# A graph layer and a routed expert layer on one core: set-up reordered, tail of expert tiles reordered, last tables in pieces

## The reference, cut to what matters

```python
# x (128, 128, 256), adj (128, 128, 128): 128 graphs of 128 nodes
def gnn(X, A):                    # X is layernorm(x)
    Xw = X @ Wv + bv
    sj, si = Xw @ aw[:d, 0], Xw @ aw[d:, 0]
    e = leaky_relu(sj[:, None, :] + si[:, :, None] + ab[0], 0.2)
    alpha = A * exp(e)
    T = alpha / (sum(alpha, -1, keepdims=True) + 1e-12)
    H, Xk = 0, X
    for k in range(3):
        H = H + Xk @ Wk[k] + bk[k]
        Xk = einsum('bij,bjd->bid', T, Xk)
    return relu(H)
def ffn(x):                       # x is layernorm(x), 16384 tokens of 256
    probs = softmax(xf @ switch_w.T + switch_b)          # 16 experts
    routes, pos = argmax(probs), rank of the token among those of its expert
    keep = pos < 1228
    y = expert_w[routes] @ token + expert_b[routes]
    return where(keep, y, xf) * max(probs)
x = x + gnn(layernorm(x))
x = x + ffn(layernorm(x))
```

## Time and profile before

| | before |
|---|---|
| median of 3 runs | 777.93 us (775.52 to 778.54) |
| the profiled execution, its own time | 778.68 us |
| its span, first to last instruction | 776.9 us |
| PE busy, PE weight loads busy | 93%, 83% of the span |
| DVE, ACT, POOL busy | 79%, 62%, 55% |
| mean granted clock of TensorE | 0.982 |

### The profile page before, as it was taken

How to read it: one execution, slowest core, us unless ns; L and a number is a source line. 1 busy time by engine, 2 the same in 40 slices (tenths; PEclk the granted TensorE clock), 3 DMA queues, 4 the chain that set the end, 5 groups by cost and what they waited for, 6 DMA issues and landing times.

```text
span 776.9 us, 18809 instructions
## 1 busy us (share of the span) xinstructions
PE 723.0 (93%) x4919; PEld 643.6 (83%) x4919; DVE 611.5 (79%) x2974; ACT 479.7 (62%) x1504; POOL 429.6 (55%) x524
## 2 busy tenths in 40 slices
PE   1999999999999999999999999999999999857883
PEld 1788888888999999999998999989989988746663
DVE  4688888888888888888888888888888887775562
ACT  1456777766666666666666666666666666653551
POOL 5224455556555566566556555665665564565553
PEclk9999999999999999999999999999999999977998
DMA  5723443534443344444434433444443322353430
GB/s 168 205 69 107 136 152 124 177 122 140 144 126 122 126 150 145 144 151 133 145 126 144 142 119 110 142 142 137 145 139 126 103 87 91 98 161 107 123 104 1
DMA packets 92926, 99.76 MB, mean 128 GB/s; under 512 B 10445, under 2 KB 85258, under 8 KB 92822
## 3 DMA queue, kind: packets, MB, share of 16 engines
q1 hardware_dynamic: 77752, 66.36, 28.5%
q0 software_dynamic: 13008, 30.07, 10.8%
q10 hardware_dynamic: 2064, 2.13, 1.0%
HBM read 49.53 MB, written 54.72 MB: 134 GB/s over the span
## 4 chain that ended last, share of the span: by engine, by line
PE 90%; DVE 2%; issue 2%; DMA 2%; SPq 1%; ACT 1%; POOL 1%; POOLq 0%; DVEq 0%; ACTq 0%
PE ps_z12a L1161 12%; PE ps_z12b L1161 11%; PE ps_z0a L1161 9%; PE ps_lgb L1161 9%; PE ps_z0b L1161 8%; PE ps_lga L1255 6%; PE ps_z0b L1262 4%; PE ps_z0a L1262 4%; PE ps_xt L1195 4%; PE ps_z12b L1221 4%; PE ps_xt L1189 4%; PE ps_z12a L1221 3%; PE ps_lgb L1295 3%; PE ps_t L1243 2%; PE ps_t L1212 2%
## 5 line engine op out<-in xcount | busy, mean ns | idle before, releaser
L529 POOL DMA_INDIRECT out<-lent,tok x143 | 145.2, 1016 | 178.2 <-DVE lent L1122 166.7
L512 POOL DMA_INDIRECT rowbuf<-rows,idx x128 | 129.6, 1013 | 55.1 <-issue 27.1
L577 ACT CAST xth<-ps_xt 128x256 fp32r<-128x256 f32 x128 | 47.7, 373 | 137.0 <-PE ps_xt L1195 136.9
L754 DVE TENSOR_TENSOR xtl<-ps_xt,xth 128x256 fp32r<-128x256 f32 x128 | 54.3, 424 | 61.1 <-ACT xft L580 59.7
L651 ACT ACTIVATE x<-rin 128x256 f32<-128x256 f32 x143 | 86.8, 608 | 2.8 <-DMA rin<-rowbuf 2.8
L1255 PEld LDWEIGHTS ps_lga<-swc,xft 128*128 128x128 f32 x512 | 76.5, 190 | 13.9 <-ACT xft L580 3.0
L480 POOL TENSOR_SCALAR x<-xin,nm,r 128x256 f32<-128x256 f32 x128 | 72.3, 565 | 27.2 <-PE ps_xt L1195 16.2
L593 ACT ACTIVATE od<-rows,oc,oa 128x256 f32<-128x256 f32 x128 | 77.0, 602 | 0.1
L476 POOL TENSOR_TENSOR r<-ve,mhalf 128x4 f32<-128x4 f32 x32 | 34.1, 1067 | 77.1 <-ACT ve L623 77.1
L1255 PE MATMUL ps_lga<-swc,xft 128*128 128x16 f32 x512 | 65.8, 242 | 2.6 <-ACT xft L580 2.6
L1195 PE MATMUL ps_xt<-ident,x 128*128 128x128 f32 x256 | 49.5, 276 | 9.2 <-POOL x L480 8.3
(11 more groups left out here) (211 smaller groups left out, 2403.9 us busy)
## 6 DMA issues: line engine op xcount, KB each, us to landing
rin<-rowbuf SPq DMA_DIRECT2D x143, 130.0 KB, 2.1
xin<-in_x SPq DMA_DIRECT2D x32, 512.0 KB, 3.9
out<-od SPq DMA_DIRECT2D x32, 512.0 KB, 4.3
ain<-in_adj SPq DMA_DIRECT2D x32, 256.0 KB, 4.3
ewr<-in_ewT SPq DMA_DIRECT2D x16, 256.0 KB, 2.7
out<-lent,tok POOLq DMA_INDIRECT x143, 2.7
rowbuf<-rin ACTq DMA_DIRECT2D x1, 2080.0 KB, 9.7
rowbuf<-rows,idx POOLq DMA_INDIRECT x128, 3.0
```

Of the source, the lines that this page charges most:

```text
L512: pool.indirect_dma_start(out=rowbuf, out_offset=bass.IndirectOffsetOnAxis(ap=idx[:, i:i + 1], axis=0), in_=rows[:, r, :], in_offset=None, ...
L529: pool.indirect_dma_start(out=out.rearrange("g n d -> (g n) d"), out_offset=bass.IndirectOffsetOnAxis(ap=tok[:, i % RY:i % RY + 1], axis=0 ...
L754: dve.tensor_tensor(xtl[:, g % 2, :], ps_xt[:, 0:D], xth[:, g % 2, :].bitcast(F32), ALU.subtract).then_inc(s_x0l, 1)
```

## The change

Set-up. SP no longer issues the loads of the weights Wk: three loads of 256 KB go out from ACT's queue at its start, each for both halves. The one semaphore `d_w` becomes four. SP then issues the first expert's weights ahead of its wait for the bias rows. ACT runs one Exp on a constant at the start and does its first slots before the two casts of `w12h`. DVE does the statistics of graphs 0 and 1 ahead of its wait for the small vectors, moves the bias rows to the end of the set-up, behind the statistics of graph 4, and cuts `w12l` in two. POOL runs one `pow` on constants (`first`) ahead of its tables of constants and of the memset of `ebp` (line 553). PE waits for `bvb` later.

Tail. PE does `expert(i)` and then `turn(i + 2)`; ACT `high(i + 1)`, `norm(i + 2)`; DVE `low(i + 1)`, `finish(i)`. For tail tiles the register load of tile i+1 stands among the products of tile i, behind the second, and three values are kept from it with `snap`; woven tiles load theirs where they did, and also with `snap`. `last_step` is cut in three pieces, behind tiles 99 to 101, `last_tiles` in six, behind tiles 102 to 107.

```diff
@@ sync
-            for kt in range(KT):
-                ks = slice(kt * P, (kt + 1) * P)
-                sp.dma_start(w12r[:, kt, 0:D], Wk[2, ks, :]).then_inc(d_w, 16)
-                sp.dma_start(w12r[:, kt, D:2 * D], Wk[1, ks, :]).then_inc(d_w, 16)
-                sp.dma_start(w0r[:, kt, 0:D], Wk[0, ks, :]).then_inc(d_w, 16)
...
             sp.dma_start(ebr[:], eb).then_inc(d_eb, 16)
-            sp.wait_ge(s_vc, KT + 4)
+            load_expert(0)
+            sp.wait_ge(s_bkl, 1)
             sp.dma_start(bkh[1:2, :].bitcast(F32), bkl[0:1, :].bitcast(F32)).then_inc(d_bkh, 16)
             load(2, 2)
-            load_expert(0)
@@ gpsimd
+            pool.tensor_tensor(first[:], onesf[:, 0:G], mhalf[:], ALU.pow)
             pool.iota(done[:], pattern=[[1, E]], base=0, channel_multiplier=0,
@@ scalar
-            act.wait_ge(s_fill, 1)
-
-            act.wait_ge(d_w, 16 * (3 * KT + 4))
-            act.copy(w12h[:], w12r).then_inc(s_wh, 1)
+            w12d = [Wk[2].rearrange("(t p) d -> p t d", p=P), Wk[1].rearrange("(t p) d -> p t d", p=P)]
+            for h in range(2):
+                act.dma_start(w12r[:, :, h * D:(h + 1) * D], w12d[h]).then_inc(d_w12, 16)
+            act.dma_start(w0r[:, :, 0:D], Wk[0].rearrange("(t p) d -> p t d", p=P)).then_inc(d_w0, 16)
+            act.wait_ge(s_pc, 2)
+            act.activation(e1[:, 0, 0:1], onesf[:, 0:1], ACT.Exp)
...
             def tile(i):
+                if i + 1 < NT:
+                    high(i + 1)
                 if i + 2 < NT:
-                    high(i + 2)
-                if i + 3 < NT:
-                    norm(i + 3)
-
-            phase_a(act, slot_fn, -LEAD_STATS, LAG_OUT)
+                    norm(i + 2)
+
+            for k in range(-LEAD_STATS, G - LEAD_STATS + 1):
+                slot_fn(0, k)
+            act.wait_ge(d_w12, 32)
+            for kt in range(KT):
+                act.copy(w12h[:, kt, :], w12r[:, kt, :]).then_inc(s_wh, 1)
+            phase_a(act, slot_fn, G - LEAD_STATS + 1, LAG_OUT)
@@ vector
             def set_up():
...
+                dve.wait_ge(d_w0, 16)
                 dve.wait_ge(s_pe0, 1)
...
                 link(dve.tensor_copy(w0h[:], w0r))
-                link(dve.tensor_tensor(w0l[:], w0r, w0h[:].bitcast(F32), ALU.subtract))
-
+                dve.wait_ge(s_wh, 1)
+                dve.tensor_tensor(w12l[:, 0, :], w12r[:, 0, :], w12h[:, 0, :].bitcast(F32),
+                                  ALU.subtract).then_inc(s_w12l, 1)
+                dve.tensor_tensor(w0l[:], w0r, w0h[:].bitcast(F32), ALU.subtract).then_inc(s_w0l, 1)
+                dve.wait_ge(s_wh, 2)
+                dve.tensor_tensor(w12l[:, 1, :], w12r[:, 1, :], w12h[:, 1, :].bitcast(F32),
+                                  ALU.subtract).then_inc(s_w12l, 1)
...
             def tile(i):
-                if i + 2 < NT:
-                    low(i + 2)
+                if i + 1 < NT:
+                    low(i + 1)
                 finish(i)
+                turn = i - (WOVEN + LAG_ROUTE + 1 - REST - G)
+                if 0 <= turn < 3:
+                    last_step(NG - 1, turn)
+                if 3 <= turn < 9:
+                    last_tiles(turn - 3)
 
             dve.wait_ge(s_pc, 13)
+            for k in range(-LEAD_STATS, -LEAD_STATS + 2):
+                slot_fn(0, k)
             dve.wait_ge(d_v, 16 * 4)
             for t in range(KT):
                 link(dve.tensor_scalar(bvb[:, t, :], onesf[:], bvt[:, t:t + 1], None, ALU.mult))
-
-            for k in range(-LEAD_STATS, -LEAD_STATS + G + 1):
+            for k in range(-LEAD_STATS + 2, -LEAD_STATS + G + 1):
                 slot_fn(0, k)
             set_up()
+            dve.wait_ge(d_x[1], 16)
+            dve.bn_stats(st1[:, G % 2, :], xin[:, G, :]).then_inc(s_st1, 1)
+            bias_rows()
@@ tensor
+            def expert_of(i):
+                pe.wait_ge(s_tab, step_of(i))
+                e = pe.value_load(tab_exp[0:1, i:i + 1], min_val=0, max_val=E - 1)
+                at[i] = [pe.snap(e * EW + t * D) for t in range(KT)], pe.snap(e * D)
+
+            def expert(i, ahead=None):
...
-                pe.wait_ge(s_tab, step_of(i))
-                e = pe.value_load(tab_exp[0:1, i:i + 1], min_val=0, max_val=E - 1)
+                if i < WOVEN:
+                    expert_of(i)
+                w, bias = at.pop(i)
                 pe.wait_ge(b_lo, i + 1)
...
+                    product(y, part, xth[:, c, ts], xtl[:, c, ts], ewh_f[:, bass.ds(w[t], D)],
+                            ewl_f[:, bass.ds(w[t], D)], start=(part == 0 and t == 0))
+                    if ahead is not None and (part, t) == (0, 1):
+                        expert_of(ahead)
...
             def tile(i):
+                expert(i, i + 1 if i + 1 < NT else None)
                 if i + 2 < NT:
                     turn(i + 2)
-                expert(i)
```

More of the change, by code:

```diff
@@ L103, in graph_then_experts @@
         abt = sb("abt", [P, 1])
+        first = sb("first", [P, G])
         cvec = sb("cvec", [P, NV])
@@ L206, in graph_then_experts @@
         d_v = sem("d_v")
-        d_w = sem("d_w")
+        d_w12 = sem("d_w12")
+        d_w0 = sem("d_w0")
+        d_bk = sem("d_bk")
+        d_r = sem("d_r")
+        s_w12l = sem("s_w12l")
+        s_w0l = sem("s_w0l")
+        s_bkl = sem("s_bkl")
         d_bkh = sem("d_bkh")
@@ L636, in slot_fn @@
                 if it * BODY + k == B + 1:
-                    for i in range(3):
+                    for i in range(2):
                         norm(WOVEN + i)
                 if it * BODY + k == B + REST:
-                    for i in range(2):
-                        high(WOVEN + i)
+                    high(WOVEN)
                 i = tailed(it, k)
@@ L814, in slot_fn @@
                 g = k + LEAD_STATS
-                if valid(it, g):
+                if valid(it, g) and it * BODY + g != G:
                     if g % G == 0:
@@ L861, in slot_fn @@
                 if s == B + REST:
-                    for i in range(2):
-                        low(WOVEN + i)
+                    low(WOVEN)
                 i = tailed(it, k)
@@ L866, in slot_fn @@
                     tile(i)
-                if s == B + LAG_ROUTE - 1:
-                    last_step(NG - 1)
-                if s == B + LAG_ROUTE:
-                    last_tiles()
             NRO = 11
@@ L1059, in advanced, with last_step, last_tiles @@
                 dve.tensor_tensor(done[:], want[:], have[:], ALU.min).then_inc(s_pick, 1)
-            def last_step(c):
-                backlog(c)
-                whole_tiles(c)
-                running(c)
-                starts(c)
-                passed(c)
-                rises(c)
-                steps(c)
-                picked(c)
-                tile_rows(c)
-                tile_experts(c)
-                reached(c)
-                limits(c)
-                advanced(c)
-            def last_tiles():
+            def last_step(c, turn):
+                if turn == 0:
+                    backlog(c)
+                    whole_tiles(c)
+                    running(c)
+                    starts(c)
+                    passed(c)
+                if turn == 1:
+                    rises(c)
+                    steps(c)
+                    picked(c)
+                    tile_rows(c)
+                    tile_experts(c)
+                if turn == 2:
+                    reached(c)
+                    limits(c)
+                    advanced(c)
+            def last_tiles(turn):
                 def link(n, ins):
@@ new lines, in last_tiles @@
+                if turn == 3:
+                    link(10, dve.tensor_reduce(base[:], pick, AX_X, ALU.add))
+                    link(11, dve.tensor_tensor(kept[:, 0:E], count, most[:], ALU.min))
+                    link(12, dve.tensor_tensor(fall[:], kept[:, 0:E], kept[:, 1:1 + E], ALU.subtract))
+                if turn == 4:
+                    link(13, dve.tensor_tensor(pick, past, by_expert(fall[:], LASTS), ALU.mult))
+                    link(14, dve.tensor_reduce(stop[:], pick, AX_X, ALU.add))
@@ L1312, in expert @@
                     ts = slice(t * P, (t + 1) * P)
-                    w = bass.ds(e * EW + t * D, D)
-                    product(y, part, xth[:, c, ts], xtl[:, c, ts], ewh_f[:, w], ewl_f[:, w],
-                            start=(part == 0 and t == 0))
-                pe.matmul(y, two_ones[:], ebp[:, bass.ds(e * D, D)], start=False, stop=True,
+                    product(y, part, xth[:, c, ts], xtl[:, c, ts], ewh_f[:, bass.ds(w[t], D)],
+                            ewl_f[:, bass.ds(w[t], D)], start=(part == 0 and t == 0))
+                    if ahead is not None and (part, t) == (0, 1):
+                        expert_of(ahead)
+                pe.matmul(y, two_ones[:], ebp[:, bass.ds(bias, D)], start=False, stop=True,
                           skip_group_check=True).then_inc(b_y, 1)
             def tile(i):
+                expert(i, i + 1 if i + 1 < NT else None)
```

(1 more changed line is left out.)

79 lines of the change are left out of this document (43 added, 36 removed).

## The result

The changed kernel takes 771.16 us (median of 6 runs, 770.63 to 771.57) and the kernel before, measured beside it, 775.71 us: a ratio of 0.9932 (95% interval 0.9915 to 0.9949), 4.6 us by the medians and 5.3 by the ratio. The profiled execution took 771.06 us for a span of 769.3, against 778.68 and 776.9 before. The kernel before was profiled once more later (776.33 us, span 774.6), so of the 7.6 us between the first two profiles 2.4 are the spread of the kernel before.

What follows compares the result with a forecast made beforehand. PE was taken to bound the slots, leaving start, drain and tail to change: -2.1 - 2.0 - 4.6 + 1.7 = -7.0, a forecast median of 771.0 us. Its own range was 767 to 774, the whole range 765.0 to 776.5.

Steps and rivals of the forecast that it cites:

- What bounds the kernel: Whole kernel: PE bounds the slots, so changes count only before the first product, in the drain and between tail tiles.
- The set-up: Start: DVE's chain begins earlier, `xtl` of graph 0 at 19.0 instead of 21.12 us; -2.1 us.
- if landings slip by a microsecond, 1.0: Set-up: lower bound, a gain of only 1.0 us if the loads land a microsecond later.
- The collision: Set-up: `bvb` on DVE meets POOL's `ebp` memset and waits until 10.1 us; without it the gain would be 4.6.
- Products before transposes: Drain: tile 98's products fit in PE's 2.8 us wait, tile 99 starts one tile earlier, at 684.8; -2.0 us.
- Tables in pieces: Drain: DVE's tables spread over tiles 99 to 107, tile 109 starts 20.9 us behind tile 99; -4.6 us.
- The register load: Plain tail loop: load stays uncovered among products, `snap` adds 0.1 us, 1.68 a tile over 33 tiles; +1.7 us.
- Rival two: Plain tail loop: load is hidden, POOL's scatter bounds the tile at 1.28 us; 13 us more gain, 758; chance 0.06.
- The first: Set-up: `bvb` escapes the memset, 2.5 us more gain, 768.5; chance 0.17.
- The third: Drain: the tables' hole is only spread, each piece adds to its tile, -4.6 becomes 0, 775.6; chance 0.17.
- The fourth: Plain tail loop: clock falls and stays low, 2.07 us a tile, 784 over all 33 tiles; chance 0.07.

Runs made afterwards that it cites:

- The last version: Changed kernel with `Wk` behind small vectors, earlier `ebp` memset, bias rows behind `xtl`, earlier loads of graphs 8-15, last row scatters back to back: 764.70 us, ratio 0.9846.
- rows first: Changed kernel with POOL issuing the last group's four row scatters back to back, scatters of finished tiles behind them: 776.71 us, ratio 0.9972.
- two loads: Changed kernel with a second register load of the same number in each tail tile, behind the fifth product: 795.80 us, ratio 1.0223.
- normalisation ahead: Changed kernel with ACT's normalisation one tile further ahead, three tiles normalised ahead of the loop: 778.57 us, ratio 0.9999.

## Why the prediction was right in size and where its steps failed

The prediction was 771.0 us, 7.0 less than the 777.93 known then; the change is worth 4.6 to 5.3 us, and the kernel before measured beside it took 775.71. That 771.0 and 771.16 lie so close is luck: the kernel before came out 2.2 us lower than known, and the gain 1.7 to 2.4 us smaller. The stages, in us, from the three undisturbed profiles (tile 99 means the start of its products):

| stage | before, first | before, second | changed | predicted change |
|---|---|---|---|---|
| to the first product | 21.52 | 20.55 | 19.24 | -2.1 |
| to the last slot's product | 642.87 | 643.09 | 641.93 | 0 |
| to tile 99 | 22.44 | 21.11 | 19.57 | -2.0 |
| to tile 109 | 25.46 | 24.75 | 23.16 | -4.6 |
| to tile 142 | 53.73 | 54.13 | 54.08 | +1.7 |
| to the end of the span | 10.9 | 11.0 | 11.3 | 0 |

Against the first profile the changes add up to -7.6, against the second, which lies nearer the medians, to -5.3. The sum came out near because errors pointed both ways: the pieces gave 2.3 to 3.0 less than their term and the start up to 0.8 less, the plain loop 1.4 to 1.8 more, and the slots gave 0.9 to 1.2 that had no term.

**What bounds the kernel** held: slots bound by PE (299.69 of 300.00 us), the gains at the start and in the drain.

**The set-up, -2.1.** Measured -2.3 between the first profiles, 2.2 on average over twelve: the size was right. The path was not. The prediction had DVE's chain run from the `ebp` memset through the two `bvb` instructions and the statistics. In the traces it runs from the landing of the last small vector through PE: PE's sums for the set-up start when that vector lands (9.49 us in the changed kernel), and DVE's copy of them, `lent_w<-ps_lgb`, comes some 2.85 us behind the landing in all ten profiles with the new set-up, whatever the memset did to `bvb`. With the bias rows ahead of `xtl` the first product comes 9.8 us behind the landing in seven profiles of eight (9.6 in the eighth), with the rows behind it 8.2 in both. The landing was put at 6.5 to 7.5 us and came at 8.3 to 9.6, so "if landings slip by a microsecond, 1.0" was wrong as well: they slipped by more, and the gain stood, since the memset was never in the path. The last version issues `Wk` behind the vectors and has them at 7.02, 2.45 us earlier, and its bias rows, 1.85 us on DVE where the prediction had 1.65, stand behind `xtl`, which is worth the 1.55 between 9.77 and 8.22: these two are its 4.0 us.

The collision itself is real. In the changed kernel's first profile it did not happen, the memset having ended at 9.10; in five others with the same set-up the vectors landed earlier, and the first `bvb`, 0.29 us otherwise, lasted until just behind the memset's end. The second profile of the changed kernel, whose memset ended at 9.11 (timeline of DVE), and the second of the kernel before, whose memset ended at 8.05:

```profile
8.53 0.98 DVE L1163 TENSOR_SCALAR lent<-onesf,bvt 128x128 f32<-128x128 f32 x2 [1.36 <-DMA abt<-in_ab]
```

```profile
6.44 2.01 DVE L1133 TENSOR_SCALAR lent<-onesf,bvt 128x128 f32<-128x128 f32 x2 [6.44 <-DMA abt<-in_ab]
```

The Trainium skill states in "SBUF — State Buffer", section "SBUF: two separate sides", that a DVE instruction in a 2-port mode and one of GpSimd lock each other out for the whole instruction. These runs agree where the other instruction is the memset: 0.98, 2.01 and 2.36 us for the two with overlap, 0.61 without. The last version doesn't show it for the `pow`: there the two took 0.61 us from 7.02, with `first` at work on POOL from 6.69 to 7.73.

The price of the `pow`, 2.01 us, was misread too. In the kernel before it ran beside DVE's `w12l` (16.14 to 17.36 us) and ended 1.03 behind it; run by itself as `first` it took 1.04, and the real one behind it 1.12. So the first one costs nothing extra, and the memset moved by 1.05 us and not by 2.

**Products before transposes, -2.0.** In the trace tile 98 went ahead of the transposes of tile 100 as predicted, and tile 99 came 1.5 to 2.9 us earlier than the slots' shift explains (the third row of the table). The order is not alone in it: the first stretch at the low clock ended 3.4 us sooner after its start, so tile 99 ran at full clock, where in the kernel before it ran at the low level. How much is the order and how much the clock, no run separates. Alone the edit gained nothing, since what it gains before the tables' hole is taken back in the hole, which then begins a tile earlier. The prediction had added the two edits as if they were independent.

**Tables in pieces, -4.6.** This is the step that failed most: 23.2 us for ten tiles, not 20.9, so 1.6 to 2.3 us gained. The walk through DVE's pieces was good (less the new wait of 2.35 us the ten tiles come to 20.8, and they took 21.3 us in the version in which POOL's rows came in time), but it followed DVE, ACT and PE and left out POOL, whose scatters of rows and of finished tiles share one queue at 1.28 us each, and which was full over the whole drain. The new wait stood there, 2.35 us in front of tile 107. "PE no longer idles long enough to lose the clock a second time" was wrong too: PE was busy 3.66 of the 7.30 us before 700.3 and lost the clock for 3.4 us. The new wait is not all of that: the last version, without it, lost the clock for the same 3.4 us from 692.3, after 6.8 us in which PE was busy 4.56 and never idle for longer than 0.80.

**The register load, +1.7.** Measured 0 to +0.4 (54.08 against 54.13 and 53.73 us). The mechanism was right: the load isn't covered among products, and its place is worth nothing; a second one costs 0.56 us a tile. What was wrong was the price of `snap`, taken as 0.1 us a tile between bounds of 0 and 0.2: it adds no instruction at all, the same operations of 151 and 46 ns stand in both traces. The sum of that step doesn't follow either: 0.1 on top of 1.63 is 1.73 a tile and +3.3, the step's own upper bound; the 1.68 is worked out from nothing that it shows.

The Trainium skill gives TensorE an engine queue of 64 in "TensorE: Matmul & The Clock Gate", section "Architectural detail: the array is 16× 32×32, not 1× 128×128"; no run here shows a queue that covers the load. PE idles behind the second product in every tile, since its sequencer has nothing issued ahead. Rival two fell with that.

**The rivals.** The first did not come: `bvb` was never done ahead of the memset in the changed kernel. The third, each piece simply added to its tile, did not come either; in the run of the pieces alone the ten tiles were 2 us shorter than in the run of the set-up alone, and a stop at tile 110 took it back. The fourth, a lasting low clock in the plain loop, did not appear in any run; the longest stretch at the low level was the drain of the run with the order alone, 27 us. The range held the result.

## What to carry to other kernels

Follow each buffer that a stall waits for back through every queue that it passes, the software DMA queue too: a queue that runs without gaps is a bound, even where its engine computes nothing, and which of its entries goes first can be worth more than the work itself. Find the landing that a chain starts from before pricing what stands beside it: here a collision of 0.2 to 0.6 us cost nothing, and each microsecond of landing cost one. Two edits around the same hole are one edit: price them together. A register load in an engine whose sequencer is already full costs nearly its whole length (0.56 of 0.64 us here); merging two loads into one tile makes it worse, because the other tile is held by another loop.

## What the runs showed that was not expected

- A load of two values took 543 ns, of one 307 (302 to 312): 0.24 us for the second value.
- The first `pow` of POOL took 1.04 us in the changed kernel, on its own in the prologue, and the next one in that prologue 1.12; in the kernel before the first had taken 2.01, ending 1.03 behind DVE's `w12l`.
- In the eight runs of the first two groups of experiments (the parts alone, the load put back, the changed kernel again, rows first, two loads, normalisation ahead) the traces hold 10,057 to 10,223 semaphore events, in all other profiles 14,905 to 14,989. In those eight, DVE and ACT went on up to 6 us behind what PE's rows had done for them, always in the drain, with the waits marked "remote", and register operations of SP took up to 0.7 us in place of 0.04. The changed kernel was slower there by 5.0 us (776.19 against 771.16), the kernel before by 1.0 to 2.8 (777.88 and 778.54 against 775.71, 776.87 and 776.86). So the ratios of those runs are of a disturbed drain; the 0.9932 and the 0.9846 come from undisturbed ones. What disturbs, and what each part of the tail is worth by itself without it, stays open.
